# B and C of a selective scan projected in four column groups and stored by SyncE; softplus by pairs of channel blocks

## The chip, the cores and the metric

One Trainium2 chip, one of its cores. The metric is the device time of one launch in microseconds (us). The kernel is written instruction by instruction for each engine, with semaphores set by hand. TensorE is PE in the profile (its weight loads are PEld), VectorE is DVE, ScalarE is ACT, GpSimd is POOL and SyncE is SP.

## The reference, cut to what matters

The input is 16 sequences of 512 tokens with 256 features. Four layers follow one another: softmax attention, an FFN quantised to fp8 values, a selective scan (Mamba) block, and a mixture of 8 experts with a shared expert. The change lies in the Mamba block:

```python
xz = xn @ in_proj_w.T + in_proj_b
xc, z = jnp.split(xz, 2, axis=-1)             # 512 channels each
u = silu(conv4(xc) + conv_b)
x_db = u @ x_proj_w.T + x_proj_b              # 32 columns
B_ssm, C_ssm = jnp.split(x_db, 2, axis=-1)    # 16 states each
delta = jax.nn.softplus(u @ dt_proj_w.T + dt_proj_b)
# h = exp(delta * A) * h + delta * u * B;  y = sum over states of h * C
```

## The kernel before, in words

The 16 sequences are worked on one after another. The core of each is the scan: 16 states times four blocks of 128 channels make 64 units. For each unit ACT computes exp(delta * A) into one of two banks (L1128), POOL multiplies du by the row of B for this state (L906, four buffers), and DVE scans over the 512 tokens (L1499). PE transposes each state's result to tokens by channels (L697, four blocks of tokens), and DVE adds it times C to acc (L1489), or ACT scales it (L1112) and POOL adds it by a DMA (L892). I call the 64 units of one sequence a turn.

Between the units of a turn every engine issues pieces of other work: the late layers of the sequence before, the projections of the next one, and the attention of the one after that. Each engine has its own list of such steps. A table written out by hand, `AT`, gives each step a slot, and the engine's generator issues it after the unit with that number. An engine runs its list strictly in order.

The steps that matter here belong to the projections of the next sequence:

- `xBC_of` (PE, slot 24): four fp32 matmuls, 128 channels by 32 columns as weights, 512 tokens as moving side, with the result in 32 partitions of a bank (L560). Slots 26 to 29 then bring the first delta projection (`dt_proj(0)`, L577).
- `bs` (ACT, slot 29): adds the bias and copies the 32x512 result to SBUF, into the space that later holds `sp` of the last channel block (L1029). ACT then starts a DMA of its 16 B rows to `b_scratch` (L1031).
- `cT_of` (PE): four transposes of 32x128 (L568), from which DVE takes C (L1318).
- `raw_of(m)` (ACT, slots 29, 37, 45, 51): Relu into delta, Abs into sp (L1049, L1050). The last waits until B is stored and C is taken.
- `exp_of(m)` (ACT, slots 36, 49, 49, 52): Exp of -sp (L1054). At slot 56 come four Ln (L1064), around which ACT loads a table twice.
- POOL adds sp to delta for each channel block (slots 57, 57, 60, 63; L845). The first four units of the next turn need delta, block by block, on ACT and on POOL (du, L900).

SP's queue loads the rows of B back, each spread over 128 partitions, into three buffers (L742). The row of state n waits until POOL has used the row of state n - 3, so it is asked for two states, or 8 units, before its use:

```python
if n >= NROW:
    sp_.wait_ge(S("dbu_ready"), 1 + (n - NROW + 1) * MC)
sp_.dma_start(bbc[:, n % NROW, :], bd[n:n + 1, :]...)
```

Before the first turn the first sequence's attention and projections run without a scan beside them. After the last turn comes the experts' stage, which the change does not touch.

## Time and profile before

| what | value |
|---|---|
| runs | 3205.36, 3212.65 and 3218.43 us; median 3212.65 us |
| the profiled execution, first to last instruction | 3209.8 us |
| PE busy | 2844.6 us (89%) |
| DVE busy | 2499.2 us (78%) |
| ACT busy | 2069.5 us (64%) |
| POOL busy | 2156.8 us (67%) |

The span of the profiled execution stands 2.9 us below the median of the runs and within their spread of 13 us. The profile gives no time around its span. The turns run from about 149 us to 2540 us of the span; the shares of the whole span therefore mix them with the experts' stage. Busy times of matmuls count their modelled ends, so neighbours overlap a little.

### The profile page before, as it was taken

What the parts mean: (1) busy time and instruction counts of PE and PEld (TensorE: products, weight loads), DVE (VectorE), ACT (ScalarE), POOL (GpSimd) and SP (SyncE); (2) the same over time, 40 slices, a digit from 0 to 9 for tenths busy, and PEclk for the clock granted to TensorE, in tenths of its full rate; (3) what the DMA queues carried; (4) which work ended last, traced back from release to release, by engine and by line L of the source; (5) the groups of instructions that cost most, each with busy time, mean ns of one, the idle gap of its engine ahead of it and who ended that gap; (6) DMA issues with size and microseconds to landing.
All of it is one profiled execution on the core that took longest, in us unless ns stands there. A gap on an engine that the chain in (4) does not pass through costs nothing. (4 is left out here: it accounts for less than half of the span.)

```text
span 3209.8 us, 46551 instructions
## 1 busy us (share of the span) xinstructions
PE 2844.6 (89%) x12888; PEld 1859.2 (58%) x12889; DVE 2499.2 (78%) x4116; ACT 2069.5 (64%) x3802; POOL 2156.8 (67%) x2205
## 2 busy tenths in 40 slices
PE   4777989898989898989899898989797789999998
PEld 2445555656555565656565655555555457777776
DVE  3499999999999999999999999999998632222222
ACT  3577777776867677777777767777675324444443
POOL 1378787787777787868696868777787514444443
PEclk7898999898999999999999999999997889999999
DMA  2043434343434343434343343434347323333333
GB/s 78 20 93 82 96 83 99 76 103 79 103 79 96 81 99 86 102 75 99 82 99 87 98 88 84 103 79 103 79 106 183 99 53 63 62 62 62 63 62 52
DMA packets 146010, 272.75 MB, mean 85 GB/s; under 512 B 19042, under 2 KB 76707, under 8 KB 145827
## 3 DMA queue, kind: packets, MB, share of 16 engines
q0 software_dynamic: 57984, 152.21, 26.6%
q1 hardware_dynamic: 77202, 109.26, 10.7%
q10 hardware_dynamic: 10640, 9.09, 0.9%
q8 instruction: 85, 1.39, 0.2%
q14 instruction: 99, 0.80, 0.1%
HBM read 107.29 MB, written 45.76 MB: 48 GB/s over the span
## 5 line engine op out<-in xcount | busy, mean ns | idle before, releaser
L906 POOL TENSOR_TENSOR dbu<-du,bbc 128x512 f32<-128x512 f32 x1024 | 1340.4, 1393 | 140.4 <-DVE h L1499 132.3
L1499 DVE TENSOR_TENSOR_SCAN h<-bank,dbu 128x512 f32<-128x512 f32 x1024 | 1223.2, 1211 | 59.3 <-ACT bank L1128 54.9
L1128 ACT ACTIVATE bank<-region,amat 128x512 f32<-128x512 f32 x1024 | 702.1, 689 | 89.6 <-DVE h L1499 84.6
L697 PE MATMUL bank<-ident,h 128*128 128x128 f32 x4096 | 621.6, 287 | 121.6 <-DVE acc L1489 51.3
L697 PEld LDWEIGHTS bank<-ident,h 128*128 128x128 f32 x4096 | 494.1, 147 | 402.8 <-issue 151.1
L1112 ACT ACTIVATE hTc<-bank,cT 128x512 f32<-128x512 f32 x448 | 306.5, 684 | 255.8 <-PE bank L697 145.9
L1666 POOL DMA_INDIRECT out<-ye,ids x136 | 213.7, 1571 | 347.3 <-DMA out<-ye,ids 312.0
L1489 DVE SCALAR_TENSOR_TENSOR acc<-bank,cT,acc 128x512 f32<-128x512 f32 x576 | 416.6, 730 | 22.9 <-PE bank L697 20.5
L892 POOL DMA_DIRECT2D acc<-hTc x224 | 203.3, 908 | 292.4 <-ACT hTc L1112 282.2
L651 PE MATMUL bank<-x4T,w_su 128*128 128x512 f32 (+1 forms) x768 | 378.5, 614 | 9.5 <-ACT region L953 8.5
L1702 DVE SCALAR_TENSOR_TENSOR gg<-gt,bank 128x352 f32<-128x352 f32 x136 | 70.7, 520 | 386.8 <-ACT gt L1636 386.8
L1603 PE MATMUL bank<-region,xeT 128*128 x1088 | 347.0, 462 | 1.5 <-ACT xeT L1632 1.5
L551 PE MATMUL bank<-region 128*128 128x512 f32 x512 | 269.7, 626 | 1.6 <-ACT region L1002 1.3
L577 PE MATMUL bank<-u,region 128*128 128x512 f32 x512 | 256.9, 596 | 0.0
L1603 PEld LDWEIGHTS bank<-region,xeT 128*128 128x128 f32 x1088 | 197.0, 191 | 89.6 <-issue 3.9
L663 PE MATMUL bank<-w_sd,shh 128*128 128x256 f32 (+1 forms) x768 | 199.4, 394 | 12.6 <-DVE shh L1425 12.6
L651 PEld LDWEIGHTS bank<-x4T,w_su 128*128 128x128 f32 (+1 forms) x768 | 127.8, 189 | 128.2 <-issue 109.4
L1619 PE MATMUL bank<-region,hT 128*128 (+1 forms) x816 | 199.2, 380 | 1.7 <-ACT hT L1641 1.7
L663 PEld LDWEIGHTS bank<-w_sd,shh 128*128 128x128 f32 (+1 forms) x768 | 132.8, 190 | 65.3 <-issue 27.2
L879 POOL DMA_INDIRECT slots_in<-x,pos x128 | 130.5, 1020 | 57.0 <-issue 26.6
L478 PE MATMUL bank<-region 128*128 128x512 f32 x256 | 159.6, 751 | 2.2 <-ACT region L946 1.8
L1647 ACT ACTIVATE ye<-bank,slot_tag 128x256 f32<-128x256 f32 x136 | 64.5, 474 | 146.8 <-PE bank L1619 143.3
(222 smaller groups left out, 4323.8 us busy)
## 6 DMA issues: line engine op xcount, KB each, us to landing
acc<-hTc POOLq DMA_DIRECT2D x224, 512.0 KB, 4.8
bbc<-b_scratch SPq DMA_DIRECT2D x256, 256.0 KB, 3.5
xe<-slots_in SPq DMA_DIRECT2D x136, 129.0 KB
region<-in_x SPq DMA_DIRECT2D x16, 512.0 KB, 3.8
out<-x ACTq DMA_DIRECT2D x16, 512.0 KB, 3.3
region<-in_e_gu SPq DMA_DIRECT2D x8, 704.0 KB, 6.1
out<-ye,ids POOLq DMA_INDIRECT x136, 3.9
slots_in<-dbu SPq DMA_DIRECT2D x16, 129.0 KB, 2.5
```

Source lines behind the costliest of these rows:

```text
L551: last = mm(proj[f"in{m}", b][:, :], w_in[:, c, m * P:(m + 1) * P], r4T[:, c, :], start=c == 0, stop=c == DC - 1)
L577: last = mm(proj[f"dt{m}", b][:, :], w_dt[:, k, m * P:(m + 1) * P], u[:, k, :], start=k == 0, stop=k == MC - 1)
L651: last = mm(late[f"{name}{n}", b][0:size, :], w_su[:, c, half * SI + at:half * SI + at + size], x4T[:, c, :], start=c == 0, stop=c == DC - 1)
L663: last = mm(late[f"d{k}", b][:, (j % 2) * D:(j % 2 + 1) * D], shh[0:size, n, j * P:(j + 1) * P], w_sd[0:size, n, :], start=n == 0, stop=n ...
L697: last = tr(scan[f"hT{s}.{t}"][:, m * P:(m + 1) * P], h[:, s % 2, m, t * P:(t + 1) * P], ident[:, :])
L906: g.tensor_tensor(dbu[:, n % 4, :], du[:, m, :], bbc[:, (b * NS + s) % NROW, :], ALU.mult).then_inc(S("dbu_ready"), 1)
L1112: f(hTc[:, s % NSENT, t - SENT[0], :], scan[f"hT{s}.{t}"][:, :], ACT.Copy, scale=cT[:, par, t, s:s + 1]).then_inc(S("scaled"), 1)
L1128: f(db(n)[:, :], delta[:, 1 - par, m, :], ACT.Exp, scale=amat[:, m, s:s + 1]).then_inc(S("da_ready"), 1)
L1489: v.scalar_tensor_tensor(acc[:, t, :], hT[:, :], c, acc[:, t, :], ALU.mult, ALU.add).then_inc(S("acc_ready"), 1)
L1499: v.tensor_tensor_scan(h[:, s % 2, m, :], db(n)[:, :], dbu[:, n % 4, :], 0.0, ALU.mult, ALU.add)\
L1603: last = mm(banks[2 * k + half][:, 0:I], xeT[:, k, c, :], w_gu[:, bass.ds(e, 1), c, half * I:(half + 1) * I].rearrange("p a n -> p (a n)") ...
L1666: g.indirect_dma_start(out, bass.IndirectOffsetOnAxis(ids[:, k:k + 1], 0), ye[:, k, :], None, compute_op=ALU.add)\
```

## The change

B and C are projected with the tokens in four blocks of 128. For each of the four channel blocks k, four matmuls write the same bank, each to its own 32 partitions (32 columns of the array): 16 matmuls of 128 tokens in place of four of 512, and all of them in slot 24. ACT's copy becomes 128x128 in place of 32x512, with the bias repeated four times, and one 128x128 transpose takes the place of four of 32x128. The store of B moves from ACT's queue to SP's and becomes four DMAs of 16 partitions by 128 tokens, between the load of row 9 and that of row 10.

For softplus, Exp, Ln and the sum are done for two channel blocks (128x1024) at a time: two Exp at slots 49 and 52, two Ln at slot 56, two sums at slots 58 and 62. The users of delta wait for its pair.

```diff
--- before.py
+++ after.py
@@ -23,6 +23,7 @@
 UNITS = NS * MC
 NROW = 3
 NX2 = 3
+STORE_AT = 10
 ADDS = [(s, t) for s in range(NS) for t in range(TT)]
 SENT, LAST_SENT, NSENT = (2, 3), NS - 2, 1
 POOLED = [(s, t) for s, t in ADDS if t in SENT and s < LAST_SENT]
@@ -196,7 +197,7 @@
         cwh, cbh = sb("cwh", [P, MC, TAPS]), sb("cbh", [P, MC])
         cwsum, cbias = sb("cwsum", [P, MC, TAPS]), sb("cbias", [P, MC])
         edge = sb("edge", [P, MC, TAPS - 1])
-        xb_all = sb("xb_all", [2 * NS, 1])
+        xb_all = sb("xb_all", [P, 1])
         dt_b, dpar = sb("dt_b", [P, MC]), sb("dpar", [P, MC])
         ddiag = sb("ddiag", [P, MC, P])
         alog, amat = sb("alog", [P, MC, NS]), sb("amat", [P, MC, NS])
@@ -232,7 +233,7 @@
         ch, sp = cs[:, 0:2, :], cs
         u = sb("u", [P, MC, T])
         du = sb("du", [P, MC, T])
-        bs = cs[0:2 * NS, MC - 1, :]
+        bs = cs[:, MC - 1, 0:P]
         cT = sb("cT", [P, 2, TT, NS])
         bbc = sb("bbc", [P, NROW, T])
         dbu = sb("dbu", [P, 4, T])
@@ -275,13 +276,13 @@
                    inv_ready=1, probT_ready=TT, x1_ready=2, xb_ready=1, q_ready=1, qT_ready=1, yb_ready=2, yb2_ready=2,
                    x2_ready=1, res_ready=1, r4_ready=1, r4T_ready=DC, zh_ready=MC,
                    zt_ready=MC, zs_ready=MC, conv_first=MC, conv_tap=MC * (TAPS - 1), conv_ready=MC, conv_tanh=MC,
-                   u_ready=MC, dt_raw=MC, dt_exp=MC, dt_ln=MC, delta_ready=MC, du_ready=MC, bs_ready=1,
+                   u_ready=MC, dt_raw=MC, dt_exp=2, dt_ln=2, delta_ready=2, du_ready=MC, bs_ready=1,
                    b_stored=1, cT_ready=1, da_ready=UNITS, dbu_ready=UNITS,
                    scan_done=UNITS, acc_init=TT, acc_ready=len(KEPT), scaled=len(POOLED), y3_ready=MC,
                    x3_ready=2, x4_ready=1, x4T_ready=DC, lexp_ready=1, sg1_ready=1, sg_ready=1, tag_ready=1, pos_ready=1, tok_set=1, weight_set=1,
                    sht_ready=len(SC), sgate_ready=len(SC), su_ready=len(SC), fin_ready=2, out_stored=1,
                    **{group: len(steps) for group, steps in SHARED.items()})
-        UNIT = {"x_loaded": 16, "b_stored": 16, "out_stored": 16}
+        UNIT = {"x_loaded": 16, "b_stored": 16 * TT, "out_stored": 16}
         b_row = [sem(f"b_row{k}") for k in range(NROW)]
         sent = sem("sent")
         dispatched = [sem(f"dispatched{w}") for w in range(2)]
@@ -317,8 +318,8 @@
             g_pe=(19, 19, 21, 38, 52, 53), g=(20, 25, 33, 40, 53, 54), gate=(22, 27, 34, 42, 55, 56), u_pe=(23, 30, 32, 35, 46, 54),
             up=(26, 33, 35, 43, 55, 56), d_pe=(53, 58), fin=(60, 64), stats3=0, rstd3=0, res=5, r4=4, r4T_pe=3, r4T=0, in_x=(6, 9, 11, 20),
             tap=(9, 10, 13, 22), conv=(11, 13, 16, 24), tanh=(12, 16, 18, 24), u=(14, 19, 21, 25), xBC_pe=24, bs=29, cT_pe=21, cT=31,
-            in_z=(30, 31, 43, 49), z=(33, 41, 48, 52), zs=(36, 45, 53, 54), dt_pe=(26, 33, 39, 48), raw=(29, 37, 45, 51), sp_exp=(36, 49, 49, 52),
-            sp_ln=56, delta=(57, 57, 60, 63), stats1=4, rstd1=2, xn=8, xT=(8, 10), xl=(9, 11), scores=(12, 16, 21, 22), maxs=(15, 20, 24, 26),
+            in_z=(30, 31, 43, 49), z=(33, 41, 48, 52), zs=(36, 45, 53, 54), dt_pe=(26, 33, 39, 48), raw=(29, 37, 45, 51), sp_exp=(49, 52),
+            sp_ln=56, delta=(58, 62), stats1=4, rstd1=2, xn=8, xT=(8, 10), xl=(9, 11), scores=(12, 16, 21, 22), maxs=(15, 20, 24, 26),
             probs=(14, 22, 24, 25), probT_pe=(27, 33, 34, 36), probT=(28, 33, 35, 37), av=(42, 46), x1=(48, 52), stats2=14, rstd2=51, xb=53, q=54,
             q_dve=56, qT_pe=23, qT=61, ffn_pe=(60, 63), ffn=(63, 64), biased_pe=(53, 64), biased=(63, 64), y_pe=(3, 4), x2=64, store=0, tags=(26, 53),
             q_round=30, q_nan=56, q_fin=58)
@@ -555,18 +556,17 @@
                     done(pe, "u_ready", b)
                     proj.may_fill(pe, "xBC", b, done)
                     for k in range(MC):
-                        if k == 2:
-                            yield 1
-                        last = mm(proj["xBC", b][0:2 * NS, :], w_x[:, k, :], u[:, k, :], start=k == 0, stop=k == MC - 1)
+                        for t in range(TT):
+                            last = mm(proj["xBC", b][t * 2 * NS:(t + 1) * 2 * NS, 0:P], w_x[:, k, :], u[:, k, t * P:(t + 1) * P],
+                                      start=k == 0, stop=k == MC - 1)
                     last.then_inc(proj.fill_sem("xBC", b), 1)
+                    yield 0
 
                 def cT_of():
                     done(pe, "bs_ready", b)
                     proj.may_fill(pe, "cT", b, done)
                     pe.sem_inc(waited_pe, 1)
-                    for t in range(TT):
-                        last = tr(proj["cT", b][:, t * 2 * NS:(t + 1) * 2 * NS], bs[:, t * P:(t + 1) * P], ident[0:2 * NS, 0:2 * NS])
-                    last.then_inc(proj.fill_sem("cT", b), 1)
+                    tr(proj["cT", b][:, 0:P], bs[:, :], ident[:, :]).then_inc(proj.fill_sem("cT", b), 1)
                     yield 0
 
                 def dt_proj(m):
@@ -734,9 +734,16 @@
             for k, (at, size) in enumerate(SC):
                 sp_.dma_start(w_sd[0:size, k, :], a["s_dn"][at:at + size, :]).then_inc(w_sloaded, 16)
 
+            def store_b(b):
+                done(sp_, "bs_ready", b)
+                for t in range(TT):
+                    sp_.dma_start(bd[b * NS:(b + 1) * NS, t * P:(t + 1) * P], bs[t * 2 * NS:t * 2 * NS + NS, :]).then_inc(S("b_stored"), 16)
+
             def rows(b, states):
                 for s in states:
                     n = b * NS + s
+                    if s == STORE_AT and b < NB - 1:
+                        store_b(b + 1)
                     if n >= NROW:
                         sp_.wait_ge(S("dbu_ready"), 1 + (n - NROW + 1) * MC)
                     sp_.dma_start(bbc[:, n % NROW, :], bd[n:n + 1, :].rearrange("a t -> (a t)").partition_broadcast(P))\
@@ -750,6 +757,7 @@
                 rows(b, range(loads_after or NROW, NS))
 
             load(1)
+            store_b(0)
             for b in range(NB - 2):
                 turn(b, b % 2, loads_after=NROW)
             turn(NB - 2, 0, loads_after=None)
@@ -839,10 +847,11 @@
                 done(pool, "rstd4", b)
                 g.tensor_tensor(s34[:, :], rstd[:, 2, :], r34[:, :], ALU.mult).then_inc(S("scale4"), 1)
                 g.tensor_tensor(b34[:, :], shift[:, 2, :], r34[:, :], ALU.mult).then_inc(S("bias4"), 1)
-                for m in range(MC):
-                    yield AT["delta"][m]
-                    done(pool, "dt_ln", b, m)
-                    g.tensor_tensor(delta[:, 1 - par, m, :], delta[:, 1 - par, m, :], sp[:, m, :], ALU.add).then_inc(S("delta_ready"), 1)
+                for k in range(2):
+                    yield AT["delta"][k]
+                    done(pool, "dt_ln", b, k)
+                    both_m = delta[:, 1 - par, 2 * k:2 * k + 2, :]
+                    g.tensor_tensor(both_m, both_m, sp[:, 2 * k:2 * k + 2, :], ALU.add).then_inc(S("delta_ready"), 1)
 
             def late_of(b, par):
                 yield AT["rstd5"]
@@ -896,7 +905,7 @@
                     if n < MC:
                         if n == 0:
                             before(pool, "dbu_ready", b)
-                        done(pool, "delta_ready", b, m)
+                        done(pool, "delta_ready", b, m // 2)
                         g.tensor_tensor(du[:, m, :], delta[:, 1 - par, m, :], u[:, m, :], ALU.mult).then_inc(S("du_ready"), 1)
                         done(pool, "du_ready", b, m)
                     if m == 0:
@@ -1026,9 +1035,7 @@
                 proj.filled(act, "xBC", b)
                 before(act, "b_stored", b)
                 before(act, "cT_ready", b)
-                f(bs[:, :], proj["xBC", b][0:2 * NS, :], ACT.Identity, bias=xb_all[:, 0:1]).then_inc(S("bs_ready"), 1)
-                done(act, "bs_ready", b)
-                act.dma_start(bd[bass.ds(b * NS, NS), :], bs[0:NS, :]).then_inc(S("b_stored"), 16)
+                f(bs[:, :], proj["xBC", b][:, 0:P], ACT.Identity, bias=xb_all[:, 0:1]).then_inc(S("bs_ready"), 1)
 
 
                 def z_of(m):
@@ -1049,19 +1056,20 @@
                     f(delta[:, 1 - par, m, :], proj[f"dt{m}", b][:, :], ACT.Relu, bias=dt_b[:, m:m + 1])
                     f(sp[:, m, :], proj[f"dt{m}", b][:, :], ACT.Abs, bias=dt_b[:, m:m + 1]).then_inc(S("dt_raw"), 1)
 
-                def exp_of(m):
-                    done(act, "dt_raw", b, m)
-                    f(sp[:, m, :], sp[:, m, :], ACT.Exp, scale=-1.0).then_inc(S("dt_exp"), 1)
-
-                steps = [(AT["raw"][m], 1, raw_of, m) for m in range(MC)] + [(AT["sp_exp"][m], 0, exp_of, m) for m in range(MC)]
-                steps += [(AT["z"][m], 2, z_of, m) for m in range(MC)]
+                def exp_of(k):
+                    done(act, "dt_raw", b, 2 * k + 1)
+                    f(sp[:, 2 * k:2 * k + 2, :], sp[:, 2 * k:2 * k + 2, :], ACT.Exp, scale=-1.0).then_inc(S("dt_exp"), 1)
+
+                def ln_of(_):
+                    for k in range(2):
+                        done(act, "dt_exp", b, k)
+                        f(sp[:, 2 * k:2 * k + 2, :], sp[:, 2 * k:2 * k + 2, :], ACT.Ln, bias=1.0).then_inc(S("dt_ln"), 1)
+
+                steps = [(AT["raw"][m], 1, raw_of, m) for m in range(MC)] + [(AT["sp_exp"][k], 0, exp_of, k) for k in range(2)]
+                steps += [(AT["z"][m], 2, z_of, m) for m in range(MC)] + [(AT["sp_ln"], 4, ln_of, 0)]
                 for at, _, step, m in sorted(steps, key=lambda x: x[:2]):
                     yield at
                     step(m)
-                yield AT["sp_ln"]
-                done(act, "dt_exp", b)
-                for m in range(MC):
-                    f(sp[:, m, :], sp[:, m, :], ACT.Ln, bias=1.0).then_inc(S("dt_ln"), 1)
 
             def late_of(b, par):
                 if b > 0:
@@ -1123,7 +1131,7 @@
                 for n in range(UNITS):
                     s, m = divmod(n, MC)
                     if n < MC:
-                        done(act, "delta_ready", b, m)
+                        done(act, "delta_ready", b, m // 2)
                     before(act, "scan_done", b, n - 1)
                     f(db(n)[:, :], delta[:, 1 - par, m, :], ACT.Exp, scale=amat[:, m, s:s + 1]).then_inc(S("da_ready"), 1)
                     if n >= LAG:
@@ -1729,7 +1737,7 @@
         x=L0_attn_x, w_lhs=column(L0_attn_w_lhs), w_rhs=column(L0_attn_w_rhs), kernel=L0_ffn_kernel, s_in=L0_ffn_input_scale,
         s_k=L0_ffn_kernel_scale, fbias=L0_ffn_bias, norm_w=column(L1_attn_norm_w), norm_b=column(L1_attn_norm_b),
         w_in=t(L1_attn_in_proj_w), in_b=column(L1_attn_in_proj_b), conv_w=L1_attn_conv_w, conv_b=column(L1_attn_conv_b),
-        w_x=t(L1_attn_x_proj_w), x_b=np.asarray(L1_attn_x_proj_b).reshape(2 * NS, 1),
+        w_x=t(L1_attn_x_proj_w), x_b=np.tile(np.asarray(L1_attn_x_proj_b), TT).reshape(P, 1),
         w_dt=t(L1_attn_dt_proj_w), dt_b=column(L1_attn_dt_proj_b), a_log=L1_attn_A_log, d_param=column(L1_attn_D_param),
         w_out=t(L1_attn_out_proj_w), out_b=L1_attn_out_proj_b,
         w_gate=np.concatenate([t(L1_ffn_gate_w), t(L1_ffn_shared_expert_gate_w)], 1),
```

## Rows read from the trace of the kernel before

**Rows 1.** The page: busy time of the span; PE's granted clock in 40 slices, in tenths.

```profile
PE 2844.6 (89%) x12888; PEld 1859.2 (58%) x12889; DVE 2499.2 (78%) x4116; ACT 2069.5 (64%) x3802; POOL 2156.8 (67%) x2205
...
PEclk7898999898999999999999999999997889999999
```

**Rows 2.** Windows, one turn each: start:end, length, busy by engine, clock, DMA.

```profile
875.00:1028.92 153.92, 139.45 (x647) 88.07 (x646) 144.96 (x228) 113.92 (x195) 119.49 (x120) 0.96 0.39 90
1028.92:1179.70 150.78, 135.85 (x643) 86.57 (x643) 144.77 (x228) 114.15 (x196) 119.50 (x120) 0.98 0.40 92
...
1485.03:1639.44 154.41, 140.31 (x645) 89.54 (x645) 145.18 (x228) 113.94 (x195) 119.56 (x120) 0.94 0.39 89
```

**Rows 3.** Windows: the two parts of one turn; PE, PEld, DVE, ACT, POOL.

```profile
1179.70:1259.70 80.00, 68.19 (x351) 47.78 (x350) 75.62 (x117) 56.44 (x97) 62.51 (x66) 0.91 0.34 80
1259.70:1331.70 72.00, 70.59 (x294) 40.69 (x295) 69.02 (x112) 57.61 (x99) 56.97 (x54) 1.00 0.46 104
```

**Rows 4.** Waits of DVE in 284:2390 (fourteen turns): us, times, longest.

```profile
DVE h L1499 <- ACT bank L1128: 41.2, 59, 2.0
```

**Rows 5.** Timeline of DVE in one turn: instructions that found it idle.

```profile
1252.39 1.22 DVE L1499 TENSOR_TENSOR_SCAN h<-bank,dbu 128x512 f32<-128x512 f32 x1 [1.98 <-ACT bank L1128]
1271.55 2.43 DVE L1499 TENSOR_TENSOR_SCAN h<-bank,dbu 128x512 f32<-128x512 f32 x2 [0.30 <-ACT bank L1128]
1286.98 1.22 DVE L1499 TENSOR_TENSOR_SCAN h<-bank,dbu 128x512 f32<-128x512 f32 x1 [0.68 <-ACT bank L1128]
1298.69 0.75 DVE L1489 SCALAR_TENSOR_TENSOR acc<-bank,cT,acc 128x512 f32<-128x512 f32 x1 [0.33 <-PE bank L697]
1329.21 0.68 DVE L1425 TENSOR_TENSOR shh<-bank,shh 64x512 f32<-64x512 f32 x1 [0.66 <-PE bank L651]
```

**Rows 6.** Timeline, all engines, around the projection of B and C.

```profile
1265.91 3.62 PE L560 MATMUL bank<-u,w_x 128*32 128x512 f32 x8
1266.36 0.11 PEld L560 LDWEIGHTS bank<-u,w_x 128*32 128x32 f32 x1 [0.32 <-issue]
...
1270.15 0.69 ACT L1112 ACTIVATE hTc<-bank,cT 128x512 f32<-128x512 f32 x1 [1.01 <-PE bank L697]
...
1273.85 0.66 ACT L1029 ACTIVATE region<-bank,xb_all 32x512 f32<-32x512 f32 x1
...
1274.55 0.35 ACTq L1031 DMA_DIRECT2D b_scratch<-region  x1
...
1275.23 0.43 PE L568 MATMUL bank<-ident,region 32*128 32x32 f32 x4
1275.34 0.69 ACT L1049 ACTIVATE region<-bank,dt_b 128x512 f32<-128x512 f32 x1 [0.82 <-PE bank L577]
```

**Rows 7.** Timeline: sixteen fp32 matmul instructions with 128 moving columns.

```profile
1205.07 2.02 PE L687 MATMUL bank<-ddiag,u 128*128 128x128 f32 x16 [0.88 <-DVE region L1333]
```

**Rows 8.** Timeline of ACT: two instructions of 1024 columns, four of 512.

```profile
1175.74 1.13 ACT L965 ACTIVATE region<-region,rs_up 128x1024 f32<-128x1024 bf16 x1
...
1176.78 1.14 ACT L966 ACTIVATE region<-region,rs_in 128x1024 f32<-128x1024 bf16 x1
...
1180.99 2.19 ACT L1064 ACTIVATE region<-region 128x512 f32<-128x512 f32 x4
```

**Rows 9.** Timeline of POOL: two sums to delta, and a very small operation.

```profile
1191.76 2.77 POOL L845 TENSOR_TENSOR region<-region 128x512 f32<-128x512 f32 x2
...
1208.52 0.20 POOL L818 TENSOR_TENSOR shift<-nought,shift 128x4 f32<-128x4 f32 x1
```

**Rows 10.** SP's queue in the same turn, and landing of ACT's store.

```profile
1274.65 7.62 SPq L742 DMA_DIRECT2D bbc<-b_scratch  x2
...
DMA to landing us min/median/max: 1.6/3.0/4.4
```

**Rows 11.** Timeline before the first turn: the sums, then ACT's first Exp of the scan.

```profile
136.14 4.94 POOL L845 TENSOR_TENSOR region<-region 128x512 f32<-128x512 f32 x4 [6.40 <-ACT region L1064]
...
148.39 1.30 ACT L1128 ACTIVATE bank<-region,amat 128x512 f32<-128x512 f32 x2
```

## The prediction

> **What bounds the kernel now.** I read the page first. It says that PE is the busiest engine, 89% of the span, and DVE next with 78% [rows 1]. That is a mean over two stages, so I cut the scan stage into turns, by the windows view between ACT's table loads. A turn lasts 150.8 to 154.4 us; from 875.00 to 1485.03 four of them take 610.0 us, 152.5 each. DVE is busy for about 145 us of each and PE for 136 to 140, so both are nearly full and ACT and POOL have slack, 38 and 33 us [rows 2]. Next I cut one turn in two at the place just ahead of the change. Up to 1259.70 PE is busy for 68 of 80 us with a granted clock of 0.91; from there to the end it is busy for 70.6 of 72 us at full clock, and DVE for 69.0 [rows 3]. The projection of B and C, the delta projections, Exp and Ln all lie in this second part. There PE has no slack and DVE next to none.
>
> The waits of DVE say what PE time can be worth. Its largest wait in fourteen turns is for ACT's exp, 41 us, 2.9 per turn [rows 4]. The timeline shows the places. The largest, 1.98 us, comes before the projection of B and C and cannot be helped by it. After it four remain: 0.30, 0.68, 0.33 and 0.66 us, 1.97 in all [rows 5]. The first follows directly from the change's place: PE starts the projection at 1265.91 and spends 3.62 us on it, ACT waits 1.01 us for a transpose behind it, and the exp behind that is late [rows 6]. So a gain behind this place ends at about 2.0 us per turn, 15 x 2.0 = 30 us; then DVE alone bounds. A loss has no such end.
>
> **PE, projection.** Before: 8 instructions (each fp32 product is two), one each 0.11 + 0.32 = 0.43 us, 3.44 us, and 0.18 for the last one's end [rows 6]. After: 16 products, 32 instructions of 128 columns. The nearest row, sixteen instructions of 128 columns at full clock, takes 2.02 us; without the same end that is 0.115 each [rows 7], 32 x 0.115 = 3.68. A quarter of 0.43 gives 3.44. One behind the other they thus cost 0 to 0.24 us more. No row shows products in different column groups. The lower bound, if they run side by side: the two instructions of a product go to the same group and follow each other, and the second can run beside the next group's first, so 16 x 0.115 = 1.84; the quickest pairs of load and matmul in the trace, four in 0.43 - 0.18 us, 0.063 each [rows 6], make 32 x 0.063 = 2.0. So 1.4 us less at best. The upper bound: no load hidden, each 0.11 us [rows 6], 32 x (0.115 + 0.11) = 7.2, or 3.8 us more. I take one behind the other, 3.5 to 3.7, as the trace shows only that.
>
> The Trainium skill, in "TensorE: Matmul & The Clock Gate", section "Part 3: Packing small matmuls", states that a weight load overlaps matmuls in flight only where the row group differs; all 32 use the same rows, and by that rule the sum would be the upper bound. The trace disagrees where groups are full width: loads of one row group are hidden at 0.115 us per pair [rows 7]. That no row shows it for narrow groups keeps it a rival.
>
> **PE, transpose.** Before 0.25 us without its end, after one instruction of 128 columns, 0.115: 0.14 less. It still waits for ACT's copy, now of a quarter of the columns. With the projection PE comes out between 0.14 less and 0.1 more per turn. Sequences 1 to 15 are projected within turns: 15 x -0.14 = -2 to +2 us.
>
> **ACT, copy and DMA.** The copy costs 0.66 us and the issue of the store 0.35 [rows 6]. A quarter of the columns can save no more than 0.66; with the issue at most 1.0 us per turn. What hides it: directly behind them ACT waits 0.82 us for PE's first delta projection [rows 6], and this wait grows as the copy shrinks. I cost it at -0.1 us per turn for the Exp behind it, between 0 and -0.3: -1.5 us in all. If the cover were gone, 0.2 us more would come out of it.
>
> **ACT, Exp and Ln by two blocks.** Two operations of 1024 columns start 1.04 us apart; four Ln of 512 take 2.19 us, and two of 1024 take 1.04 + 1.14 = 2.18 [rows 8]. So a column costs the same in either form, and nothing is gained on ACT. The first Exp moves from slot 36 to 49 and the last doubles, so 0.5 us more stand in slot 52 between scan exps; ACT runs two units ahead, and it has slack. Cost 0, at most 0.2 per turn.
>
> **POOL, sums.** Two take 2.77 us; an operation of 4 columns takes 0.20, the most a merge can save [rows 9]: 0 to 0.4 us per turn, on an engine with 33 us of slack. Delta's first pair comes one unit later, the second at the turn's end, together with what used to stand there; du of the first unit has the same four sums in front of it. Cost 0.
>
> **SP, store.** SP stands behind row 9 and now waits for ACT's copy, which ends at 1274.51 [rows 6]. Row 10 was issued at 1274.65 anyway [rows 10]. The four stores delay it by about 4 x 0.35 = 1.4 us; it was asked for 8 units, about 19 us, before its use. B lands 1.6 to 4.4 us after issue [rows 10], and the last Abs that waits for it is at slot 51, 20 units later. Queued behind the waiting SP are row loads and the load of x only. Cost 0; an unhidden delay of row 10 would cost at most 1.4 per turn.
>
> **Before the first turn.** Delta waits for a pair of Ln, 0.5 us, and the last Exp likewise. POOL's sums take 4.94 us from 136.14, and ACT starts the scan's first Exp only at 148.39, after the attention of the next sequence [rows 11]. Cover 7 us: cost 0 to 1.
>
> **The sum.** Own span 3209.8: PE 0 (-2 to +2), ACT -1.5, the beginning +0.5 at most, together about -2: 3208. The runs have their median 2.9 us above that span, so on their scale it is about 3210; I put 3208, between, since the cases of gain outweigh for small amounts. The likeliest case's own range is 3197 to 3222, chance 0.50.
>
> **Rivals.**
> 1. *Column groups run side by side* (0.25). PE gives back 1.4 + 0.14 us, less than the 1.97 us of DVE's idle behind it, of which perhaps 1.2 to 1.4 comes out: 15 x 1.3 = 19 us, 3193. For it: the order is made for it, four neighbours in four groups. Against: both halves of an fp32 product need the same group, and no row shows it. The Trainium skill, in "TensorEngine Tiling (Array Packing)", section "Key Properties", says that tiles load and multiply in parallel, which would make this case.
> 2. *The other side: narrow loads aren't hidden* (0.12). 3.8 us more per turn on a PE that is busy for 98% of that part [rows 3]. It decides against the change as soon as an instruction takes over 0.15 us, that is 1.1 us more per turn; at 0.225 it is 15 x 3.7 = 56 us, 3268. Half of it gives 3240.
> 3. *The clock decides* (0.13). The turns differ by 3.6 us with the same instructions: 150.8 us at a mean clock of 0.98, 154.4 at 0.94 [rows 2]. The low clock stands in the first part, where PE pauses [rows 3]. A turn of another length moves the pauses. If all fell like the longest, 15 x 1.9 = 29 us more; like the shortest, 26 less. Half of either is likelier: 3198 or 3227.
> 4. *The stores or their 512-byte rows get in the way of the accumulating DMAs*: contained in the ranges above.
>
> **How the numbers follow.** 0.5% is 16 us, about what a measurement can tell from no change. Faster than 3196.6: 0.6 of rival 1, a third of rival 3, a little of the main case: 0.15 + 0.04 + 0.04 = 0.23. Slower than 3228.7: rival 2 and under half of rival 3, 0.11 + 0.05 = 0.16. Within: 0.61. The range, 3188 to 3236, leaves out the full rival 2 (about 0.10) and the lower end of rivals 1 and 3 (0.08).
>
> **What would show it.** L560 in the timeline: 32 instructions in 3.6 to 3.9 us confirm the main case, about 2.2 rival 1, about 7 rival 2. ACT's 1.01 us wait behind it goes with that. Two Exp and two Ln of about 1.14 us each. SP's four stores end before 1276 on the scale of this turn, and POOL never waits for a row of B. Turn lengths, beside the mean clock, show rival 3. The prediction is wrong if DVE's idle time per turn changes by more than 1 us, whatever engine it is put down to.

## The result, and the profile after

The changed kernel takes 3194.32 us (median of 8 runs, 3187.29 to 3207.09) where the kernel before takes 3217.65 (8 runs): ratio 0.9932, 95% interval 0.9919 to 0.9945, so 0.7% or about 22 us faster. The same kernel measured again (after_again) gave 0.9924 (0.9904 to 0.9944). The profiled execution took 3194.2 us, 1.8 more than its span of 3192.4; the span is 17.4 below the one of before.

The page of the changed kernel, to be held against [rows 1]:

```profile
PE 2801.8 (88%) x13224; PEld 1852.8 (58%) x13225; DVE 2491.5 (78%) x4116; ACT 2055.7 (64%) x3738; POOL 2155.1 (68%) x2173
...
PEclk8898999999999899999999999989998799999999
```

PE has 336 instructions more and 43 us less busy time. The timeline of the changed kernel around the projection of B and C, to be held against [rows 6]:

```profile
1255.90 1.08 PE L560 MATMUL bank<-u,w_x 128*32 128x128 f32 x32
...
1256.91 0.66 PE L697 MATMUL bank<-ident,h 128*128 128x128 f32 x4
...
1257.77 0.69 ACT L962 ACTIVATE region<-bank,nmax 128x512 f32<-128x512 f32 x1 [0.68 <-DVE nmax L1242]
...
1258.69 1.10 PE L577 MATMUL bank<-u,region 128*128 128x512 f32 x2 [1.12 <-ACT region L962]
...
1263.02 0.35 ACT L1038 ACTIVATE region<-bank,xb_all 128x128 f32<-128x128 f32 x1
...
1263.39 2.36 SPq L740 DMA_DIRECT2D b_scratch<-region  x4
...
1263.95 0.27 PE L569 MATMUL bank<-ident,region 128*128 128x128 f32 x1
1264.15 0.69 ACT L1056 ACTIVATE region<-bank,dt_b 128x512 f32<-128x512 f32 x1 [0.79 <-PE bank L577]
...
1265.79 0.42 SPq L749 DMA_DIRECT2D bbc<-b_scratch  x1
```

Three things are to be seen. The 32 instructions take 1.08 us; without the 0.27 us of the last one, that is 0.026 from one start to the next. PE goes on at 1256.91, 1.01 us after it began; before, it went on after 3.55. Right behind that PE waits 1.12 us, which it did not before: the first delta projection needs a bank that ACT's Exp of the last attention scores (L962) has yet to read. And ACT still waits 0.79 us for that delta projection, so what its copy saved is hidden. Both waits stand in every turn from the second to the thirteenth, the one for the bank with 1.02 to 1.13 us.

The waits of DVE in the same window as [rows 4], 284:2390, and in one turn as [rows 5], behind the projection:

```profile
DVE h L1507 <- ACT bank L1136: 27.5, 35, 2.0
```

```profile
1275.61 1.22 DVE L1507 TENSOR_TENSOR_SCAN h<-bank,dbu 128x512 f32<-128x512 f32 x1 [0.27 <-ACT bank L1136]
1287.32 0.75 DVE L1497 SCALAR_TENSOR_TENSOR acc<-bank,cT,acc 128x512 f32<-128x512 f32 x1 [0.18 <-PE bank L697]
1300.36 2.41 DVE L1507 TENSOR_TENSOR_SCAN h<-bank,dbu 128x512 f32<-128x512 f32 x2 [0.73 <-ACT bank L1136]
1317.95 0.68 DVE L1426 SCALAR_TENSOR_TENSOR shh<-bank,shh 64x512 f32<-64x512 f32 x1 [0.34 <-ACT bank L1104]
1318.79 0.68 DVE L1433 TENSOR_TENSOR shh<-bank,shh 64x512 f32<-64x512 f32 x1 [0.16 <-PE bank L651]
1320.06 1.29 DVE L1268 TENSOR_SCALAR bank<-region 128x512 int32<-128x512 int32 x2 [0.59 <-ACT region L975]
```

The waits of 0.30 and 0.68 us behind the projection shrank to one of 0.27, but 44 us behind it a new one of 0.73 us for ACT stands. The last three rows are the turn's end, where one wait of 0.66 for PE has become three, two of them for ACT. So in this turn the waits behind the projection did not shrink in sum, 1.97 us before and 2.27 now, and from the projection's start to the next table load it takes 65.90 us where the turn of [rows 6] takes 65.82. Other turns gained, as the means below show, and waits are only a part of what they gained. Another part is a small comparison of DVE (`ohb`, 128x64, for the router of the experts), about 11 us behind the projection's start. Before and after, POOL's row first:

```profile
1275.50 2.79 POOL L906 TENSOR_TENSOR dbu<-du,bbc 128x512 f32<-128x512 f32 x2
1277.69 0.68 DVE L1381 TENSOR_TENSOR ohb<-iota,f 128x64 f32<-128x64 f32 x1
```

```profile
1265.54 1.57 POOL L915 TENSOR_TENSOR dbu<-du,bbc 128x512 f32<-128x512 f32 x1
1267.18 0.22 DVE L1389 TENSOR_TENSOR ohb<-iota,f 128x64 f32<-128x64 f32 x1
```

Before, it starts under a multiplication of POOL, which ends at 1278.29, and itself ends 0.08 us later. In the changed kernel POOL's ended at 1267.11, just ahead of it, and it takes 0.22 us. Of the 224 comparisons in the traces of all fourteen kernels, 116 start under a multiplication of POOL and end 0.08 to 0.21 us behind it; the other 108 take 0.22 to 0.23 us. The view counts the difference, 0.4 us per turn, as busy time of DVE and not as waiting.

Turns differ in length with their mean clock, now even more than before, as windows of one turn each show (compare [rows 2]):

```profile
1168.47:1321.80 153.33, 137.95 (x666) 89.00 (x665) 144.42 (x228) 112.92 (x191) 119.54 (x119) 0.94 0.39 90
1321.80:1469.83 148.03, 132.40 (x665) 85.02 (x665) 143.94 (x228) 113.27 (x191) 119.26 (x118) 0.99 0.41 93
2075.21:2231.01 155.80, 140.11 (x665) 91.48 (x665) 144.84 (x228) 112.94 (x192) 119.27 (x118) 0.92 0.38 89
```

So I cut every turn in two, for all kernels: from ACT's load of the Ln table to the start of the projection (the first part, with the low clock), and from there to the next table load (the second part, at full clock). Means are over the 13 turns from the second to the fourteenth. The turns of one kernel scatter by 0.4 to 0.8 us in the second part and by 0.8 to 2.5 in the first (standard deviations), so a mean is good to 0.1 to 0.2 us there and to 0.2 to 0.7 in the first. The last two columns are read in the second part: DVE's idle time, and the length of the comparison.

| kernel | PE from the projection's start to its next work | first part | second part | ratio to before (95%) | DVE idle | comparison |
|---|---|---|---|---|---|---|
| before | 3.55 us | 86.3 | 66.18 | 1 | 3.16 | 0.65 |
| changed | 1.01 | 86.3 | 65.23 | 0.9932 (0.9919 to 0.9945) | 2.83 | 0.23 |
| the same again (after_again) | 1.01 | 85.8 | 65.21 | 0.9924 (0.9904 to 0.9944) | 2.76 | 0.23 |
| proj_only | 1.01 | 86.5 | 64.91 | 0.991 (0.9891 to 0.993) | 2.54 | 0.22 |
| soft_only | 3.55 | 85.7 | 66.53 | 1.000 (0.9985 to 1.0015) | 3.47 | 0.66 |
| pairs | 1.47 | 86.2 | 65.27 | one run, 3192.74 us | 2.88 | 0.24 |
| serial | 2.39 | 86.4 | 65.21 | 0.995 (0.9936 to 0.9965) | 2.86 | 0.23 |
| thrice | 2.76 | 87.0 | 65.64 | 0.9951 (0.9934 to 0.9967) | 3.10 | 0.41 |
| quad | 3.63 | 86.5 | 66.71 | 1.0001 (0.9985 to 1.0016) | 3.57 | 0.66 |
| one_group | 3.61 | 86.6 | 66.11 | one run, 3215.59 us | 3.14 | 0.65 |
| sp_store | 3.55 | 86.1 | 66.21 | 0.9995 (0.998 to 1.0009) | 3.20 | 0.66 |
| act_store | 1.01 | 86.1 | 66.93 | 1.002 (1.0005 to 1.0035) | 4.23 | 0.23 |
| max25 | 1.01 | 88.8 | 63.46 | 0.9956 (0.994 to 0.9973) | 2.64 | 0.65 |
| dt27 | 1.01 | 85.9 | 67.76 | 1.0043 (1.0026 to 1.006) | 5.07 | 0.23 |

Between before and changed the first part did not move beyond its scatter; the second lost 0.95 us: 0.33 of DVE's idle time, 0.42 of the comparison, and 0.2 of other DVE work that lies on the other side of the cut or ran a little quicker. Per turn 0.95 us would make 15 x 0.95 = 14 us. The spans differ by 17.4: 3.5 us ahead of the first Ln table load (130.64 in place of 134.14), 12.8 between the first and the sixteenth, and 1.1 behind it.

### The profile page after: what moved, and what is told of

Its sections match the earlier page's. It is cut to its first block and busy times, and to the rows that moved or that the text cites. A ratio compares the mean times of both kernels' runs of the same rounds, so it can differ in the third digit from the quotient of the medians.

```text
span 3192.4 us, 47175 instructions
## 1 busy us (share of the span) xinstructions
PE 2801.8 (88%) x13224; PEld 1852.8 (58%) x13225; DVE 2491.5 (78%) x4116; ACT 2055.7 (64%) x3738; POOL 2155.1 (68%) x2173
## 5 line engine op out<-in xcount | busy, mean ns | idle before, releaser
L577 PE MATMUL bank<-u,region 128*128 128x512 f32 x512 | 258.1, 598 | 13.8 <-ACT region L962 13.8
```

The lines of the kernel that those rows point to most:

```text
L577: last = mm(proj[f"dt{m}", b][:, :], w_dt[:, k, m * P:(m + 1) * P], u[:, k, :], start=k == 0, stop=k == MC - 1)
```

## The experiments

My theory after the result was: the gain is TensorE's freed time in the second part, and a part of it turned into the wait for a bank. The rivals: the softplus pairs or ScalarE's shorter copy bring a share; or it is not the groups but the shortness of the instructions.

**proj_only and soft_only: the two halves of the change.** proj_only is the changed kernel with Exp, Ln, the sums, their slots and their waits as before; soft_only is the kernel before with only these changed.

```diff
-sp_exp=(49, 52), delta=(58, 62)            # changed kernel
+sp_exp=(36, 49, 49, 52), delta=(57, 57, 60, 63)   # proj_only
...
-                    f(sp[:, 2 * k:2 * k + 2, :], sp[:, 2 * k:2 * k + 2, :], ACT.Exp, scale=-1.0)
+                    f(sp[:, m, :], sp[:, m, :], ACT.Exp, scale=-1.0)
```

> Only the projection part of the change: column groups, one transpose, four stores on SyncE; Exp, Ln and the sum stay by single channel blocks. Theory A (the gain is TensorE time freed ahead of a part of the turn where TensorE is full): the whole gain is here, ratio 0.993 to the kernel before, between 0.991 and 0.995, the part of a turn from the projection to the table load 65.2 us as in the changed kernel, 66.2 before. Rival B (the softplus pairs bring part of it): 0.996 or more. Rival C (the softplus pairs cost something, by a longer Exp between the scan's exps): below 0.992.

> Only the softplus part: Exp, Ln and sum by two channel blocks, projection and store as before. Theory A: ratio 1.000, between 0.998 and 1.002, two Ln take 2.0 to 2.2 us in all. Rival B: 0.997 or less. Rival C: 1.002 or more.

Measured: 0.991 and 1.000. The whole gain is in the projection half. 0.991 lies at the edge of theory A's range and in rival C's, and the second part was 64.91, not 65.2. That part shows a cost of the pairs twice, 66.53 - 66.18 = 0.35 and 65.23 - 64.91 = 0.32 us per turn, with a standard error of 0.11 and 0.15 from the turns taken one by one; 15 x 0.33 = 5 us, 0.15%, is below what the ratios tell apart. after_again, which was to tell whether the changed kernel is slower than proj_only, gave 0.9924, inside the 0.992 to 0.994 that I had set for such a cost, with an interval that reaches to 0.9904. ACT itself is not slower for the pairs: the two Ln of the changed kernel take 2.01 us, the four before 2.19 [rows 8].

```profile
1169.76 2.01 ACT L1066 ACTIVATE region<-region 128x1024 f32<-128x1024 f32 x2
```

**serial, pairs, one_group: are the groups side by side?** All keep 32 instructions of 128 tokens and 32 columns of weights. serial exchanges the loops, pairs alternates between two groups at a time, one_group puts all tokens into the first group of the kernel before.

```diff
-for k in range(MC):
-    for t in range(TT):
+for t in range(TT):          # serial
+    for k in range(MC):
...
+for k, t in [(k, t) for half in range(2) for k in range(MC) for t in (2 * half, 2 * half + 1)]:   # pairs
...
-last = mm(proj["xBC", b][0:2 * NS, :], w_x[:, k, :], u[:, k, :], ...)
+last = mm(proj["xBC", b][0:2 * NS, t * P:(t + 1) * P], w_x[:, k, :], u[:, k, t * P:(t + 1) * P], ...)   # one_group
```

> The changed kernel with the two loops of the projection exchanged: the four products of one column group follow one another, the same 32 instructions. Theory A with column groups side by side: only neighbours in different groups overlap, so the 32 instructions take 3.3 to 3.7 us in place of 1.08, and the ratio is 0.998 to 1.002. Rival (short instructions of 32 columns are cheap by themselves, whatever group follows): they stay near 1.1 us and the ratio stays 0.993.

> The changed kernel with the products ordered so that neighbours alternate between two groups, the first two groups first, the other two behind: if each group streams at 0.107 us per instruction and two run side by side, 32 x 0.107 / 2 = 1.7 us, less some overlap at the one change of pairs: 1.4 to 1.75 us. If any change of group is enough for full overlap: 1.0 us.

> The kernel before with its projection in the same 32 short instructions (128 tokens each), all in the first column group, all 128 partitions' worth of tokens side by side in the free dimension. If a group streams at its own pace, 0.107 us per instruction (a quarter of 0.43): 3.4 to 3.5 us, as before. In the run with the loops exchanged the same 32 instructions took 2.4 us, four groups one after the other; the difference to 3.4 is then overlap at the three changes of group. If short instructions with 32 columns of weights are quicker by themselves: 2.0 to 2.4 us.

The timelines of PE, serial first, then pairs, then one_group:

```profile
1249.23 2.46 PE L560 MATMUL bank<-u,w_x 128*32 128x128 f32 x32
1251.62 0.66 PE L697 MATMUL bank<-ident,h 128*128 128x128 f32 x4
```

```profile
1252.81 1.54 PE L559 MATMUL bank<-u,w_x 128*32 128x128 f32 x32
1254.28 0.66 PE L696 MATMUL bank<-ident,h 128*128 128x128 f32 x4
1255.60 1.10 PE L576 MATMUL bank<-u,region 128*128 128x512 f32 x2 [0.67 <-ACT region L961]
```

```profile
1265.78 3.68 PE L561 MATMUL bank<-u,w_x 128*32 128x128 f32 x32
1269.39 0.66 PE L699 MATMUL bank<-ident,h 128*128 128x128 f32 x4
```

In one group the 32 take 3.61 us, as long as eight of 512 tokens: short instructions are not cheaper by themselves, and the 32 narrow loads cost less than 0.1 us together. With two groups alternating the time is 1.47, with four 1.01, both as expected.

serial missed its expectation: 2.39, not 3.3 to 3.7. Against one_group it saved 3.61 - 2.39 = 1.22 us at three changes of group, 0.41 each. The starts of the single instructions in the trace show how. In one group they stand 0.11 us apart. In serial the first instruction of the second group starts 6 ns after the fifth of the first group, and the two groups then alternate until the first is done, so four instructions of each run side by side. In the changed kernel four instructions start within 20 ns, the next four 0.11 us later, and so on, eight times. So each group keeps its own pace of 0.11 us, and a group can start while three instructions of the group before it still have to. That they wait at their group meanwhile is my reading of these starts; no run varies it.

pairs shows the wait for the bank shrinking as the projection grows: 0.67 us in place of 1.12, and its second part is the changed kernel's.

**thrice and quad: what is a microsecond of TensorE worth?**

```diff
-for k in range(MC):
+for k in [k for _ in range(3) for k in range(MC)]:   # range(4) in quad
```

> The changed kernel with the projection of B and C done three times over in the same groups (the last result counts): 96 instructions, about 2.7 to 3.1 us, 1.7 to 2.1 us more TensorE time per turn. Theory A: the first 1.1 us of it fill TensorE's wait for a bank ahead of the first delta projection and are free, the rest costs; ratio 0.995 to 0.998. Rival (every us freed or added counts in full): 2 us x 15 = 30 us more than the changed kernel, ratio 1.002. Rival (TensorE time here does not matter at all, the gain came from ScalarE): ratio stays 0.993.

> The changed kernel with the projection of B and C done four times over in its column groups: 128 instructions, which at 0.027 us each take 3.5 us, as long as the eight of the kernel before. Everything else is the changed kernel. If the gain is TensorE's freed time alone, it is gone: 0.999 to 1.001, and the part of the turn behind the projection is 66.2 us or, with the 0.3 us of softplus by pairs, 66.5. If ScalarE's shorter copy and the issue taken from it bring a share of their own, that share stays: 0.995 to 0.998 and 65.7 to 66.0 us.

The timelines of PE in quad and in thrice:

```profile
1268.38 3.70 PE L560 MATMUL bank<-u,w_x 128*32 128x128 f32 x128
1272.02 0.65 PE L697 MATMUL bank<-ident,h 128*128 128x128 f32 x4
1272.51 1.02 PE L577 MATMUL bank<-u,region 128*128 128x512 f32 x2
```

```profile
1263.37 2.83 PE L560 MATMUL bank<-u,w_x 128*32 128x128 f32 x96
1266.12 0.66 PE L697 MATMUL bank<-ident,h 128*128 128x128 f32 x4
```

Both came out as theory A expected. quad, with TensorE's time as before and all else changed, is at 1.0001: nothing of the gain came from anything but TensorE's time. With its softplus by pairs it is to be held against soft_only, 66.71 and 66.53.

The row of second parts, 65.23 at 1.01 us, 65.21 at 2.39, 65.64 at 2.76, 66.71 at 3.63, says what the time is worth. From 1.0 to 2.4 it is worth nothing that the means can tell, since it mostly fills the wait for the bank (in serial, thrice and quad PE goes straight on to L577, without a wait). Then 0.87 us cost 1.07. Of the 1.50 us between serial and quad 0.71 is idle time of DVE and 0.42 the comparison, which starts 0.97 us into POOL's multiplication in quad and about 1.26 us into it in thrice. So a part of what PE's time is worth here depends on where the comparison meets POOL.

The ratios are coarser: serial and thrice at 0.995 lie 0.2% above the changed kernel, about 6 us, at the edge of their intervals. Of these 6, 2 us come ahead of the first turn, where nothing hides PE's time (table load at 133.06 in serial and 132.55 in thrice, 130.64 and 131.32 in the two runs of the changed kernel).

**act_store and sp_store: ScalarE's share.** act_store lets ACT issue the four stores behind its copy; sp_store is the kernel before with its one store on SP.

```diff
+done(act, "bs_ready", b)            # act_store; store_b(...) is gone from SyncE
+for t in range(TT):
+    act.dma_start(bd[b * NS:(b + 1) * NS, t * P:(t + 1) * P], bs[t * 2 * NS:t * 2 * NS + NS, :])
...
-act.dma_start(bd[bass.ds(b * NS, NS), :], bs[0:NS, :])            # sp_store
+sp_.dma_start(bd[b * NS:(b + 1) * NS, :], bs[0:NS, :])
```

> The changed kernel with its four stores of B issued by ScalarE right behind its copy, in place of SyncE: ScalarE is held for 4 x 0.35 = 1.4 us there. If the 0.7 us that ScalarE saves by the change (copy 0.66 to 0.35, issue 0.35 to 0) are hidden by its wait of 0.8 us for the first delta projection, only about 0.6 to 1 us shows on ScalarE and the ratio rises by at most 0.002, to 0.993 to 0.995. If ScalarE's time at this place is a part of the gain, 1.4 us x 15 = 21 us come back: 0.998 or more.

> The kernel before with only the store moved to SyncE's queue, still one DMA, so ScalarE saves 0.35 us of issue. If the gain is TensorE's alone: 0.999 to 1.001. If ScalarE's time counts here: 0.35 x 15 = 5 us, 0.998; if the order of the queues counts for more, 0.997 or less.

The timeline of act_store:

```profile
1275.48 2.43 ACTq L1038 DMA_DIRECT2D b_scratch<-region  x4
...
1277.96 0.69 ACT L1056 ACTIVATE region<-bank,dt_b 128x512 f32<-128x512 f32 x1 [2.51 <-issue]
...
1279.28 1.13 PE L552 MATMUL bank<-region 128*128 128x512 f32 x2 [1.51 <-ACT region L1057]
```

sp_store is at 0.9995: moving one store alone is worth nothing measurable. act_store went well beyond what I expected, 1.002, although its projection is the fast one: four stores in a row hold ACT for 2.43 us, not 1.4, longer than the 0.8 us that it has to spare there. ACT's Relu (L1056) starts 2.5 us behind the copy where in the changed kernel it waited 0.79, which is 1.7 later. PE then waits 1.51 us for the bank that ACT's Abs frees, and the second part is 1.70 us longer than in the changed kernel, 15 x 1.7 = 26 us. So ScalarE's time is free at this place up to its wait and costs in full beyond; with four stores, the move to SyncE is what keeps the gain.

**max25 and dt27: attempts at a better version**, both from proj_only.

```diff
-maxs=(15, 20, 24, 26)
+maxs=(15, 20, 24, 25)          # max25
...
-dt_pe=(26, 33, 39, 48)
+dt_pe=(27, 33, 39, 48)         # dt27
```

> An attempt at a better version: the projection part alone, and the last maximum of the scores on VectorE in slot 25 in place of 26. In the changed kernel TensorE, done with B and C, waits 1.12 us for ScalarE's Exp of the last scores, which frees the bank of the first delta projection, and that Exp waits 0.68 us for this maximum. If that wait is what the freed time turned into, it shrinks or goes and up to 1.1 us per turn more comes out, bounded by VectorE's idle time behind it of about 1.2 us: 0.985 to 0.990. If VectorE is the bound by now, 0.991 as without it; if the maximum now waits for TensorE's scores, slower.

> A second attempt at a better version: the projection part alone, and the first delta projection in slot 27 in place of 26. TensorE then has one group of four transposes, 0.43 us, to do ahead of the bank that it waits 1.12 us for, and the order in which the banks are handed out stays. If the wait is what the freed time turned into: 0.2 to 0.4 us per turn, 0.989 to 0.990 beside the 0.991 of the projection alone; if the later delta projection holds ScalarE up instead (its Relu in slot 29 waits 0.8 us for it already): 0.992 to 0.995.

Timelines of PE in max25 and in dt27:

```profile
1256.69 3.09 PE L651 MATMUL bank<-x4T,w_su 128*128 128x512 f32 x6
1261.74 1.08 PE L560 MATMUL bank<-u,w_x 128*32 128x128 f32 x32 [1.96 <-ACT region L961]
1262.75 0.66 PE L697 MATMUL bank<-ident,h 128*128 128x128 f32 x4
1263.24 1.02 PE L577 MATMUL bank<-u,region 128*128 128x512 f32 x2
```

```profile
1271.76 0.66 PE L697 MATMUL bank<-ident,h 128*128 128x128 f32 x4
1274.41 0.66 PE L697 MATMUL bank<-ident,h 128*128 128x128 f32 x4 [2.00 <-DVE acc L1495]
```

In max25 the earlier slot also changed which bank each step gets, since the banks are handed out by these slots: the wait for the same Exp moved ahead of the projection and grew to 1.96 us, and the comparison is back at 0.65 us. The second part fell to 63.46 us, the first rose by 2.3. In dt27 the transposes that PE now does first need a bank that DVE frees only later: it waits 2.00 us where it waited 1.12. And the second case of its expectation came true, by more than I had put on it. The last piece of the delta projection moved with it to slot 30, and ACT's Relu that needs it stands in slot 29:

```profile
1281.43 0.69 ACT L1055 ACTIVATE region<-bank,dt_b 128x512 f32<-128x512 f32 x1 [3.22 <-PE bank L577]
```

In the thirteen turns this wait is 3.2 to 3.8 us, 0.8 in proj_only. DVE's idle time in the second part doubled with it, from 2.54 to 5.07. max25 at 0.9956 and dt27 at 1.0043 are both worse than any value that I had expected for them with a number. Neither beats proj_only, which has the lowest ratio and, by its second part, is 0.3 us per turn better than the changed kernel; the ratios of the two overlap.

## Why the prediction was right, point by point

- **What bounds.** Right: of what the turns gained, all lies in the second part, where PE was found full, and the first part stayed at 86.3 us. The cap of 1.97 us was read as idle time of DVE that PE's time could fill. Of the 1.27 us that proj_only gained, 0.62 was DVE's idle time; 0.43 was the comparison, which no longer runs into POOL's multiplication and whose stretch had counted as busy. So "then DVE alone bounds" left out that DVE's busy time itself depends on what POOL does at that moment. The sign at the prediction's end, that it is wrong if DVE's idle time per turn changes by more than 1 us, did not appear: over both parts it went from 7.8 to 7.4.
- **The number.** The median of 3194 lies outside the likeliest case's own range, 3197 to 3222, and inside the range as a whole, 3188 to 3236, because that range took in rival 1, with a chance of 0.25.
- **PE, projection.** Here the main case failed, the step "I take one behind the other, 3.5 to 3.7, as the trace shows only that": the four groups run side by side. The lower bound failed too. It had the two instructions of an fp32 product, which go to one group, keep the next group waiting (1.84 us), and took the quickest pairs of the trace, 0.063 us, for a floor (2.0 us). Measured were 1.01 us and 0.026 per instruction: neither limits. In the trace four instructions start within 20 ns, and each group then goes on at 0.11 us. I looked for the floor among instructions that all go to one place.
- **Rival 1** carried the result and its time of 3193 is 1 us from it, but that closeness is luck: two misses cancel, and the kernel before, whose 3212.65 the 3193 was counted from, has its median at 3217.65 over eight runs, so the gain was 22 us and not 19. PE gave back 2.54 us, not 1.4; of that, 1.27 came out with single-block softplus and 0.95 with pairs, where I had 1.3. Most of the rest went into the wait of 1.12 us for a bank, which the prediction did not have: I asked who waits behind the projection, and not what the work behind it itself waits for. In the kernel before the slow projection covered that wait. Its sign came as well: ACT's wait of 1.01 us behind the projection is gone, and in quad it is back with 1.09.
- **Rival 2** did not come: all 32 loads use the same rows and none shows, in one group (3.61 us) or in four (1.01). The Trainium skill's rule in "TensorE: Matmul & The Clock Gate", section "Part 3: Packing small matmuls", is that loads overlap matmuls in flight only where the row group differs: the trace disagrees. The Trainium skill's rule in "TensorEngine Tiling (Array Packing)", section "Key Properties", is that tiles load and multiply in parallel: the trace agrees.
- **PE, transpose.** One instruction, with ACT's copy at 0.35 us: no gain could be told apart in it; quad, which has it, is at 1.
- **ACT, copy and DMA.** Right that 0.7 us are hidden: quad and sp_store show no gain of their own. The cover was described rightly: 0.82 us of waiting before, 0.79 now that PE comes earlier too, and 1.13 in quad, where PE takes as long as before and the wait grows by the 0.31 us that the copy lost. act_store shows the price without it. The cost of issuing was wrong: 4 x 0.35 = 1.4 was 2.36 on SP and 2.43 on ACT. Row 10 went out at 1265.79, and among POOL's waits none is for a row of B, as forecast.
- **ACT, Exp and Ln by two blocks.** That a column costs the same in either form was read from two instructions of another kind, with 1.14 us each. The two Ln take 2.01 us where four took 2.19, so ACT gains 0.18 there, which the prediction had put at nothing. It was right that the turn gains nothing by it. The cost, 0 to 0.2, was measured in traces at 0.32 and 0.35 us per turn. The new waits of DVE for ACT at the end of the turn stand where it is lost, and in the same turn of proj_only they are missing: one wait of 0.66 us for PE stands there, as before. So they come with the pairs; that it is the doubled Exp in slot 52 was not tried.
- **The beginning.** Costed at 0 to +1, it came out 3.5 us shorter, and 2.8 in the second profile of the same kernel. Its projection ran for 3.62 us there too and is on the path, which I did not price.
- **The clock** (rival 3) spread the turns over 148.0 to 155.8 us, and the means of the first part differ by 0.5 us between two runs of one kernel. It decided nothing here that the traces show, but it is why 0.2% needs the second part's length and can't be read from a span.

## What to carry to other kernels

When a price is missing from the trace because no instruction there takes the new path, the nearest row is no bound for it: a floor read from work in one place says nothing of work in four. For an engine that is full, ask what comes out of every microsecond freed by reading what its next instruction waits for; the work removed was hiding that wait. What an instruction of the other full engine takes can change too when its start moves against a third engine's work: compare busy times instruction by instruction, not idle times alone. And in a kernel whose slots also hand out the buffers, a slot moved by one can cost more than the wait that it was to remove.

## What the runs showed of the hardware that I had not expected

- fp32 matmuls with 32 columns of weights, in four column groups and ordered so that neighbours differ in group, ran at 0.026 us per instruction of 128 tokens, against 0.11 in one group, with all loads hidden. The granted clock was 1.00 of full speed in the second part of the turns of these runs, the level of 2.4 GHz. Until PE's next work the 32 took 1.01 us in four groups, 1.47 with two alternating and 3.61 in one: 3.6 times as quick.
- Groups used one after the other still overlapped: 2.39 us, where one group alone took 3.61. Each change of group saved 0.41 us.
- A comparison of DVE (128x64) took 0.22 us by itself, but 0.68 where it started 1.0 us into a multiplication of POOL. In all 116 cases in which it started under one it ended 0.08 to 0.21 us behind POOL's end. The small DVE instructions around it kept their length. Why this one waits is not shown here.
- One DMA of 16 partitions (2 KB each) issued alone held ACT for 0.35 us and SP for 0.32; four in a row (512 bytes each) held SP for 2.36 and ACT for 2.43, 0.6 each.
